# The expert down projection of two steps ends in one group of matmuls, in other row quarters

## The chip, the cores and the metric

The kernel runs on one core of a Trainium2 chip, as one launch. The metric is the device time of a run in microseconds (us); the time of before is the median of three runs.

## The reference

What is computed is a stack of six stages on 1024 tokens of width 512: a feed-forward block with retrieval, an attention, the same feed-forward block, a mixture of experts, a second attention, the mixture of experts again. The change touches the mixture of experts, which occurs twice:

```python
H, F, E, K = (512, 800, 8, 2)
...
top_vals, top_idx = jax.lax.top_k(probs, K)
...
h1 = jnp.einsum('th,efh->tef', xt, w1)
h3 = jnp.einsum('th,efh->tef', xt, w3)
act = jax.nn.silu(h1) * h3
expert_out = jnp.einsum('tef,ehf->teh', act, w2)
y = jnp.einsum('te,teh->th', w_full, expert_out)
```

Each token goes to 2 of 8 experts. An expert has 800 middle columns. All is float32.

## The kernel before

**Streams and steps.** The 2048 pairs of token and expert are sorted by expert and cut into blocks of 32 rows (`SR`), each of one expert. The blocks are dealt to four streams (`NSTR`), so that a stream has 18 steps (`NSTEP`), and one step handles four blocks, one of each stream. Stream j owns the column quarter j of TensorE's array (32 of its 128 columns) and the 32 PSUM partitions from 32j on. Both occurrences (f = 0 and f = 1) together have 36 steps.

**One step p**, over the engines:

- POOL: `gather(p)` (L880) is an indirect DMA that fetches 128 token rows from `h_scratch` into one of two slots of `XB`. Its wait is for the slot to be free. The scatter (L892) writes the step's 128 result rows from `YB` to `y_scratch`; it waits for `m_yc`, which the copy of the step raises. POOL's program is: gather(0), gather(1), then for each p: gather(p+2), wait for `m_yc` of step p, scatter of step p.
- DVE: `turn_rows(p)` (L1119) turns the gathered rows with 16 transposes. For step p its program is: `turn_rows(p+1)`, the two products of step p (L1125), the transposes of the activation of step p (L1138, L1141), which raise `m_at`.
- PE: `up(p)` (L954) multiplies by w1 and w3: 64 matmuls of 400 columns. It waits for `turn_rows(p)` (`m_xt`) and for both products of step p-1 (`m_act`), whose PSUM banks it writes. `down(p)` (L972, L975) multiplies by w2. The 800 middle columns are six chunks of 128 (`FC`), 24 matmuls of 512 columns at L972, and 32 left over (`FR`), 4 matmuls at L975 that use only 32 rows of the array, here called the tail. A step writes PSUM bank 4 or 5 (`4 + u`, u = p mod 2). PE's program is: up(0), up(1), down(0), up(2), down(1), up(3), down(2), and so on.
- ACT: silu of step p (L1001, two halves), then the copy of step p-1 from PSUM to `YB` (L1007), which waits for `m_y`, raised by the tail of that step, and raises `m_yc`.
- SP: issues the weight loads. A stream keeps its weights while its expert stays the same; the load is then skipped by a condition, but the instruction is still executed. `up_in` (L794) loads w1 and w3, `down_in` (L803) the chunks of w2, `tail_in` (L810) the 32 left-over rows of w2 (64 KB) into `W2B`. `down_in` and `tail_in` of a step raise one semaphore, `w2_in`, and wait for `m_y` of the step before.

Of the kernel before, what the change touches and what calls it, by code (L numbers as in the profile page):

```python
# [14 lines left out]
P = 128  # L15
T, D = 1024, 512
# [17 lines left out]
NE, FF, TOPK = 8, 800, 2  # L34
# [14 lines left out]
def macaron_program(nc, A, out, stages=6):  # L49

    ctx = ExitStack()
    with ctx:
# [159 lines left out]
        XBT = take([2, C, P])  # L212
        AC = take([FF])
        ACT_T = take([2, FC, P])
        ACT_R = take([2, SR])
        YB = take([2, D])
        W2B = take([D])
        W2_LAST = take([FC // 2, D])
        W13, W2A = [None] * NSTR, [None] * NSTR
        for j in (2, 0, 1):  # L220
# [565 lines left out]
        yl_in = [sem(f"yl_in{i}") for i in range(NT)]  # L786
        LOADS = NSTEP + 1
        N13 = 16 * NSTR
        N2 = 16 * (2 * NSTR + 1)
        assert NSTEP % 2 == 0  # L790

        def up_in(eng, j, a, e, cond=None):

# [11 lines left out]
                              cond=cond).then_inc(w2_in, 16)  # L805
                at += n

        def tail_in(eng, j, e, cond=None):

            eng.dma_start(W2B[SR * j:SR * j + SR], A["w2b"][e].rearrange("e p d -> p (e d)"),  # L810
                          cond=cond).then_inc(w2_in, 16)

        def guess(j):

# [8 lines left out]
        def sp_moe(eng, k, f):  # L823
            h, last = HS[k][0], 2 if f == 0 else 3
            for i in range(NT):
                eng.wait_ge(s_h, NT * k + i + 1)
                eng.dma_start(HD[i * P:(i + 1) * P, :], h[:, i, :]).then_inc(S("s_hd"), 16)
            eng.wait_ge(stage_end, 4 * k)
            for j in range(NSTR):
                tail_in(eng, j, guess(j))  # L830
            eng.wait_ge(S("s_hd"), 16 * NT * (f + 1))
            eng.wait_ge(S("s_lgt"), 4 * f + 4)
            guess_in(eng, f, last)

            eng.wait_ge(S("s_eb"), f + 1)
            late = None
            for p in range(NSTEP + 1):
                if p < NSTEP:
                    now = []
                    for j in range(NSTR):  # L840
                        q = j * NSTEP + p
                        x = eng.value_load(EBX[q:q + 1, 0:1], min_val=0, max_val=2 * NE - 1)
                        now.append((bass.ds(x % NE, 1), x >= NE))
                    for a in range(2):
                        if p == 0:
                            eng.wait_ge(w13_in[a], N13 * (LOADS * f + 1))
                        elif a == 0:
                            eng.wait_ge(S("m_wf"), NSTEP * f + p)
                        else:
                            eng.wait_ge(S("m_h"), 2 * (NSTEP * f + p))  # L850
                        for j in range(NSTR):
                            up_in(eng, j, a, *now[j])
                if p >= 1:
                    if p == 1:
                        eng.wait_ge(w2_in, N2 * (LOADS * f + 1))
                    else:
                        eng.wait_ge(S("m_y"), NSTEP * f + p - 1)
                    for j in range(NSTR):
                        down_in(eng, j, *late[j])
                        tail_in(eng, j, *late[j])  # L860
                late = now
            if f == 0:
                sp_attn1_weights(eng)
            for u in range(2):
                eng.wait_ge(y_out[u], 8 * NSTEP * (f + 1))
            for i in range(NT):
                rows_back(eng, i, 0)
# [29 lines left out]
        def pe_moe(eng, k, f):  # L897
# [65 lines left out]
            def down(p):  # L963
                G, u = NSTEP * f + p, p % 2
                eng.wait_ge(w2_in, N2 * (LOADS * f + p + 2))
                eng.wait_ge(S("m_at"), G + 1)
                if G >= 2:
                    eng.wait_ge(S("m_yc"), G - 1)
                for c in range(FC):
                    for j in range(NSTR):  # L970
                        part = W2A[j][c // W2A[j][0].shape[1]]
                        eng.matmul(PS[SR * j:SR * j + SR, 4 + u, :], ACT_T[:, u, c, SR * j:SR * j + SR],  # L972
                                   part[:, c % part.shape[1], :], start=(c == 0), stop=False, skip_group_check=True)
                for j in range(NSTR):
                    mm = eng.matmul(PS[SR * j:SR * j + SR, 4 + u, :], ACT_R[SR * j:SR * j + SR, u, :],  # L975
                                    W2B[SR * j:SR * j + SR, :], start=False, stop=True, skip_group_check=True)
                mm.then_inc(S("m_y"), 1)

            for p in range(NSTEP):
                up(p)  # L980
# [7 lines left out]
        def act_moe(eng, link, k, f):  # L988
            eng.wait_ge(S("s_fall"), f + 1)
            eng.activation(LESS, FALL, ACT.Exp).then_inc(S("s_less"), 1)  # L990
            eng.wait_ge(S("s_xturn"), f + 1)
            eng.copy(XBT[:, 0], PS[:, 6, :].rearrange("p (c t) -> p c t", c=C)).then_inc(S("m_xfirst"), 1)

            for p in range(NSTEP + 1):
                G = NSTEP * f + p
                if p < NSTEP:
                    for hf in range(2):
                        eng.wait_ge(S("m_h"), 2 * G + hf + 1)
                        if G > 0:
                            eng.wait_ge(S("m_at"), G)  # L1000
                        eng.activation(AC[:, hf * FH:(hf + 1) * FH], PS[:, 2 * hf, 0:FH], ACT.Silu).then_inc(S("m_sg"), 1)  # L1001
                if p >= 1:
                    u = (p - 1) % 2
                    eng.wait_ge(S("m_y"), G)
                    if p >= 3 or f == 1:
                        eng.wait_ge(y_out[u], 16 * (NSTEP // 2 * f + (p - 1) // 2))
                    eng.copy(YB[:, u, :], PS[:, 4 + u, :]).then_inc(S("m_yc"), 1)  # L1007
            for u in range(2):
                eng.wait_ge(y_out[u], 8 * NSTEP * (f + 1))
            for i in range(NT):  # L1010
                rows_back(eng, i, 1)
            if f == 0:
                for i in range(NT):
                    act_front(eng, k + 1, i)

        def dve_moe(eng, link, k, f):
# [110 lines left out]
            for p in range(NSTEP):  # L1127
                G, u = NSTEP * f + p, p % 2
                if p + 1 < NSTEP:
                    turn_rows(p + 1)  # L1130
                product(G, 0)
                product(G, 1)
                eng.wait_ge(S("m_act"), 2 * G + 2)
                if G >= 2:
                    eng.wait_ge(S("m_y"), G - 1)
                for a in range(NSTR):
                    rows = slice(SR * a, SR * a + SR)
                    eng.transpose(ACT_R[rows, u, :], AC[rows, FC * P:FF])  # L1138
                    for b in range(NSTR):
                        src = AC[rows, 0:FC * P].rearrange("p (c f) -> p c f", c=FC)  # L1140
                        tr = eng.transpose(ACT_T[SR * b:SR * b + SR, u, :, rows], src[:, :, SR * b:SR * b + SR])  # L1141
                tr.then_inc(S("m_at"), 1)
# [548 lines left out]
```

## Time and profile before

| | |
|---|---|
| median of 3 runs | 1366.42 us (1364.42 to 1369.72) |
| profiled execution: its time, its span | 1372.15 us, 1370.4 us |
| mean granted TensorE clock | 0.937 |
| PE busy | 1185.6 us, 87% of the span |
| DVE, ACT, POOL busy | 866.3, 350.0, 123.5 us |
| PE at L954 / L972 / L975 on the chain that ended last | 28% / 13% / 2% |

The span runs from the first to the last instruction of the profiled execution, and 1.75 us lie around it. The chain that ended last is followed back from the last instruction, at each step to what released it. A float32 matmul shows as two records, so a tail of four matmuls has 8. Line numbers are those of the kernel before; the first occurrence of the experts lies at about 195 to 545 us, the second at about 990 to 1368 us.

### The profile page before, as it was taken

The page shows a single profiled execution, that of the slowest core. Times are in us where ns is not written, and L with a number is a line of the kernel's source. Part 1 is how long each engine was busy: PE and PEld are TensorE (multiplying, and loading weights), DVE is VectorE, ACT ScalarE, POOL GpSimd, SP SyncE. Part 2 cuts the span into 40 slices and gives each one's busy share as a digit, 9 for nine tenths or more (in the row PEclk, how much of TensorE's full clock was granted, in tenths as well). Part 3 has the DMA queues.
Part 4 walks back from the last instruction along what each step waited for, and adds up shares of the span by engine and source line. Part 5 has one row for each costly group of instructions (what it writes and reads, how often), then busy time and mean ns, then how long its engine had stood idle before and what let it go on. Part 6 is the DMA issues. An engine that isn't in the chain of part 4 may idle for free.

```text
span 1370.4 us, 26531 instructions
## 1 busy us (share of the span) xinstructions
PE 1185.6 (87%) x9782; PEld 486.0 (35%) x9782; DVE 866.3 (63%) x2491; ACT 350.0 (26%) x723; POOL 123.5 (9%) x151
## 2 busy tenths in 40 slices
PE   6799756999999994688789999999759889999982
PEld 3477422333333331333334444433323323333320
DVE  4731476767787763654888888841358657777753
ACT  4434420000000000121166666674100000000000
POOL 1100010111111100220100000000100111111100
PEclk9899887999999997799999999999869999999995
DMA  9000332047503244239514331005640533514545
GB/s 368 11 1 1 142 137 99 32 175 280 216 33 128 94 155 170 94 101 128 101 42 78 58 56 29 2 2 215 279 167 17 224 123 138 185 65 140 179 179 206
DMA packets 44521, 166.15 MB, mean 121 GB/s; under 512 B 7613, under 2 KB 14355, under 8 KB 40039
## 3 DMA queue, kind: packets, MB, share of 16 engines
q1 hardware_dynamic: 34415, 137.28, 30.3%
q0 software_dynamic: 5760, 18.88, 4.0%
q10 hardware_dynamic: 4216, 8.29, 2.7%
q8 instruction: 77, 1.26, 0.4%
q14 instruction: 53, 0.43, 0.1%
HBM read 786.00 MB, written 22.03 MB: 590 GB/s over the span
## 4 chain that ended last, share of the span: by engine, by line
PE 75%; DVE 12%; DMA 5%; issue 3%; ACT 3%; SPq 1%; POOL 1%; ACTq 0%; POOLq 0%; DVEq 0%
PE PS L954 28%; PE PS L972 13%; PE PS L1397 5%; PE PS L1360 4%; PE PS L1384 4%; DVE PS L1519 3%; PE PS L975 2%; PE PS L706 2%; PE PS L689 2%; PE PS L1424 2%; PE PS L1343 2%; PE PS L479 2%; PE PS L493 1%; DMA HH<-in_w 1%; PE PS L1348 1%
## 5 line engine op out<-in xcount | busy, mean ns | idle before, releaser
L954 PE MATMUL PS<-arena 128*32 128x400 f32 x3456 | 399.0, 504 | 8.0 <-DMA HH<-in_w 4.0
L954 PE MATMUL PS<-HH,arena 128*32 128x400 f32 x1152 | 398.5, 504 | 0.0
L1119 DVE STREAM_TRANSPOSE arena<-arena 32x128 f32<-32x128 f32 x544 | 164.7, 303 | 144.8 <-DMA arena<-h_scratch,RT 137.6
L954 PEld LDWEIGHTS PS<-arena 128*32 128x32 f32 x3456 | 141.4, 111 | 261.7 <-issue 257.2
L1519 DVE CUSTOM_DVE_ANT_0 PS<-PS,U 128x128 f32<-128x128 f32 (+7 forms) x256 | 188.0, 783 | 59.3 <-PE PS L1360 58.5
L1141 DVE STREAM_TRANSPOSE arena<-arena 32x192 f32<-32x192 f32 x576 | 211.4, 367 | 7.2
L972 PE MATMUL PS<-arena 128*32 128x512 f32 x1512 | 197.7, 604 | 15.0 <-DMA arena<-in_w2b 15.0
L1465 ACT ACTIVATE arena<-PS 128x512 f32<-128x512 f32 (+3 forms) x384 | 165.2, 496 | 74.0 <-PE PS L1387 48.4
L1001 ACT ACTIVATE arena<-PS 128x400 f32<-128x400 f32 x72 | 36.3, 504 | 363.4 <-PE PS L954 363.4
L954 PEld LDWEIGHTS PS<-HH,arena 128*32 128x32 f32 x1152 | 124.6, 111 | 0.0
L1360 PE MATMUL PS<-arena 96*128 96x512 bf16 (+3 forms) x384 | 104.0, 332 | 17.6 <-DVE arena L1519 13.7
L1384 PE MATMUL PS<-arena 99*128 99x512 bf16 (+3 forms) x384 | 111.9, 330 | 5.1 <-DVE arena L1503 2.2
L972 PEld LDWEIGHTS PS<-arena 128*32 128x32 f32 x1512 | 55.9, 112 | 142.9 <-issue 125.2
L972 PE MATMUL PS<-HH,arena 128*32 128x512 f32 x216 | 104.2, 621 | 0.0
L892 POOL DMA_INDIRECT y_scratch<-arena,RT x36 | 35.7, 991 | 573.7 <-ACT arena L1007 573.7
L1397 PE MATMUL PS<-arena 128*32 128x512 f32 (+3 forms) x768 | 80.2, 497 | 0.0
L1007 ACT COPY arena<-PS 128x512 f32<-128x512 f32 x36 | 21.1, 586 | 223.9 <-PE PS L975 223.9
L479 PE MATMUL PS<-ident,HH 128*128 128x128 f32 x128 | 29.0, 382 | 53.7 <-DVE HH L454 52.7
L1343 PE MATMUL PS<-HH,arena 128*128 128x512 f32 x128 | 63.6, 622 | 0.8 <-ACTq L158 0.8
L1360 PEld LDWEIGHTS PS<-arena 96*128 96x128 bf16 x384 | 31.3, 99 | 92.1 <-DVE arena L1519 62.8
L1125 DVE TENSOR_TENSOR arena<-arena,PS 128x400 f32<-128x400 f32 x72 | 39.3, 569 | 34.4 <-ACT arena L1001 33.1
L1384 PEld LDWEIGHTS PS<-arena 99*128 99x128 bf16 x384 | 37.1, 98 | 55.5 <-ACT arena L1465 34.1
(246 smaller groups left out, 1156.3 us busy)
## 6 DMA issues: line engine op xcount, KB each, us to landing
arena<-in_w SPq DMA_DIRECT2D x228, 1600.0 KB
arena<-in_w2a SPq DMA_DIRECT2D x114, 1536.0 KB
HH<-in_w SPq DMA_DIRECT2D x76, 1600.0 KB
HH<-in_w2a SPq DMA_DIRECT2D x38, 768.0 KB
arena<-in_w2a SPq DMA_DIRECT2D x38, 768.0 KB
arena<-in_w2b SPq DMA_DIRECT2D x152, 64.0 KB
arena<-split_scratch SPq DMA_DIRECT2D x72, 128.0 KB, 6.5
split_scratch<-arena SPq DMA_DIRECT2D x48, 128.0 KB, 2.3
```

The source lines that it names most:

```text
L479: tr = eng.transpose(PS[:, FB[k][i % 2], c * P:(c + 1) * P], HS[k][0][:, i, c * P:(c + 1) * P], ident[:])
L954: mm = eng.matmul(PS[SR * j:SR * j + SR, 2 * hf + m, 0:FH], XBT[:, u, c, SR * j:SR * j + SR], W13[j][:, c // 2, m, c % 2, hf * FH:(hf + 1) ...
L972: eng.matmul(PS[SR * j:SR * j + SR, 4 + u, :], ACT_T[:, u, c, SR * j:SR * j + SR], part[:, c % part.shape[1], :], start=(c == 0), stop=Fal ...
L1119: tr = eng.transpose(XBT[SR * b:SR * b + SR, u, :, SR * a:SR * a + SR], src[:, :, SR * b:SR * b + SR])
L1125: eng.tensor_tensor(half, half, PS[:, 2 * hf + 1, 0:FH], ALU.mult).then_inc(S("m_act"), 1)
L1141: tr = eng.transpose(ACT_T[SR * b:SR * b + SR, u, :, rows], src[:, :, SR * b:SR * b + SR])
L1343: mm = eng.matmul(PS[:, at + par, :], wcols[:, par], HS[k][1][:, c, J * HT_:(J + 1) * HT_], start=(c == 0), stop=(c == C - 1))
L1360: mm = eng.matmul(PS[:, b + lo // HT_, 0:hi - lo], QT[0:KS, slot, h, i * P:(i + 1) * P], KT[0:KS, slot, h, lo:hi], start=True, stop=True)
L1384: mm = eng.matmul(bank[:, 0:hi - lo], KT[0:KS + 3, slot, h, i * P:(i + 1) * P], QT[0:KS + 3, slot, h, lo:hi], start=True, stop=not diag, s ...
L1397: mm = eng.matmul(PS[32 * h:32 * h + 32, 7, lo - J * HT_:HT_], VA[:, i, (GH * g + h) * VC:(GH * g + h) * VC + 32], PB[:, n % 3, h, 0:hi - lo],
L1465: eng.activation(PB[:, (n // GH) % 3, h, 0:hi - lo], PS[:, 4 + n % 3, 0:hi - lo], ACT.Exp, scale=SCALE1).then_inc(S("s_p"), 1)
L1519: eng.tensor_tensor_reduce(scores, scores, MASKW[:, T - wide:T], 1.0, HOLE, ALU.add, ALU.max, MP[:, g % 2, h, i:i + 1]).then_inc(S("s_md"), 1)
```

## The change

The tail of an even step is not multiplied in its own `down`. It waits for the tail of the odd step after it, and both are multiplied together, 8 matmuls in turn: those of the even step in row quarter j and column quarter j, those of the odd step in row quarter j+1 (mod 4) and column quarter j, with results in banks 4 and 5. So it is for steps 0 to 15; steps 16 and 17 (`not paired`) each end with a tail of their own. What follows from it in the code:

- `ACT_R` (the left-over columns of the activation) has 4 slots instead of 2, `W2B` two buffers, one of them in `U`, which is free in this stage.
- The last L972 matmul of each step raises a new semaphore `m_w2`; `down_in` and the DVE transposes wait for that instead of `m_y`. `m_y` rises by two at the tail of a pair.
- `tail_in` comes behind all `down_in` of a step, has semaphores of its own (`w2b_in`) and no condition: 4 x 64 KB at each step.
- ACT copies both steps of a pair one after the other, behind the silu of the step after the pair.
- POOL's program, with its waits, is not edited.

```diff
-        ACT_R = take([2, SR])
+        ACT_R = take([4, SR])
         YB = take([2, D])
-        W2B = take([D])
+        W2B = [take([D]), U]
...
+        def paired(p):
+
+            return p < NSTEP - 2
+
+        def y_done(p):
+
+            return p + 2 if paired(p) and p % 2 == 0 else p + 1
+
+        def last_rows(p, j):
+
+            r = (j + p % 2) % NSTR
+            return slice(SR * r, SR * r + SR)
...
-        def tail_in(eng, j, e, cond=None):
-
-            eng.dma_start(W2B[SR * j:SR * j + SR], A["w2b"][e].rearrange("e p d -> p (e d)"),
-                          cond=cond).then_inc(w2_in, 16)
+        def tail_in(eng, p, j, e):
+
+            eng.dma_start(W2B[p % 2][last_rows(p, j)], A["w2b"][e].rearrange("e p d -> p (e d)")).then_inc(w2b_in[p % 2], 16)
...
                 if p >= 1:
-                    if p == 1:
+                    q = p - 1
+                    if q == 0:
                         eng.wait_ge(w2_in, N2 * (LOADS * f + 1))
                     else:
-                        eng.wait_ge(S("m_y"), NSTEP * f + p - 1)
+                        eng.wait_ge(S("m_w2"), NSTEP * f + q)
                     for j in range(NSTR):
                         down_in(eng, j, *late[j])
-                        tail_in(eng, j, *late[j])
+                    if q >= 2:
+                        eng.wait_ge(S("m_y"), NSTEP * f + y_done(q - 2))
+                    for j in range(NSTR):
+                        tail_in(eng, q, j, late[j][0])
...
+                mm.then_inc(S("m_w2"), 1)
+                if paired(p) and p % 2 == 0:
+                    return
+                ends = (p - 1, p) if paired(p) else (p,)
+                for q in ends:
+                    eng.wait_ge(w2b_in[q % 2], N2B * (NSTEP // 2 * f + q // 2 + 1))
                 for j in range(NSTR):
-                    mm = eng.matmul(PS[SR * j:SR * j + SR, 4 + u, :], ACT_R[SR * j:SR * j + SR, u, :],
-                                    W2B[SR * j:SR * j + SR, :], start=False, stop=True, skip_group_check=True)
-                mm.then_inc(S("m_y"), 1)
+                    for q in ends:
+                        rows = last_rows(q, j)
+                        mm = eng.matmul(PS[SR * j:SR * j + SR, 4 + q % 2, :], ACT_R[rows, (NSTEP * f + q) % 4, :],
+                                        W2B[q % 2][rows, :], start=False, stop=True, skip_group_check=True)
+                mm.then_inc(S("m_y"), len(ends))
...
-                if p >= 1:
-                    u = (p - 1) % 2
-                    eng.wait_ge(S("m_y"), G)
-                    if p >= 3 or f == 1:
-                        eng.wait_ge(y_out[u], 16 * (NSTEP // 2 * f + (p - 1) // 2))
+                if p >= 1 and not paired(p - 1):
+                    ready = (p - 1,)
+                elif p >= 2 and p % 2 == 0:
+                    ready = (p - 2, p - 1)
+                else:
+                    ready = ()
+                for q in ready:
+                    u = q % 2
+                    eng.wait_ge(S("m_y"), NSTEP * f + y_done(q))
+                    if q >= 2 or f == 1:
+                        eng.wait_ge(y_out[u], 16 * (NSTEP // 2 * f + q // 2))
                     eng.copy(YB[:, u, :], PS[:, 4 + u, :]).then_inc(S("m_yc"), 1)
```

On PE, before, at the end of down(0) of the first occurrence (the last chunks, the tail, the first matmuls of up(2)); down(1) ends in the same way:

```order
L972 MATMUL PS<-arena 32x512 x3
L972 MATMUL PS<-HH,arena 32x512
L972 MATMUL PS<-arena 32x512 x12
L975 MATMUL PS<-arena 32x512 x4
L954 MATMUL PS<-arena 32x400 x3
```

and of the change, first at the end of down(0) (L989 and L971 are the lines of before's L972 and L954):

```order
L989 MATMUL PS<-arena 32x512 x3
L989 MATMUL PS<-HH,arena 32x512
L989 MATMUL PS<-arena 32x512 x12
L971 MATMUL PS<-arena 32x400 x3
L971 MATMUL PS<-HH,arena 32x400
```

then at the end of down(1) (L1000 is the line of before's L975, `U` the second buffer of left-over rows):

```order
L989 MATMUL PS<-arena 32x512 x12
L1000 MATMUL PS<-arena 32x512
L1000 MATMUL PS<-U,arena 32x512
L1000 MATMUL PS<-arena 32x512
L1000 MATMUL PS<-U,arena 32x512
L1000 MATMUL PS<-arena 32x512
L1000 MATMUL PS<-U,arena 32x512
L1000 MATMUL PS<-arena 32x512
L1000 MATMUL PS<-U,arena 32x512
L971 MATMUL PS<-arena 32x400 x3
```

The four tail matmuls of down(0) have moved behind down(1), in turn with its own.

On ACT, from the first silu of the experts on, before (two silu halves a step, then a copy):

```order
L1001 ACTIVATE arena<-PS 128x400 x4
L1007 COPY arena<-PS 128x512
L1001 ACTIVATE arena<-PS 128x400 x2
L1007 COPY arena<-PS 128x512
L1001 ACTIVATE arena<-PS 128x400 x2
L1007 COPY arena<-PS 128x512
```

and of the change (L1026 is the silu, L1038 the copy):

```order
L1026 ACTIVATE arena<-PS 128x400 x6
L1038 COPY arena<-PS 128x512 x2
L1026 ACTIVATE arena<-PS 128x400 x4
L1038 COPY arena<-PS 128x512 x2
```

The copy of step 0 has moved from behind the silu of step 1 to behind that of step 2, next to the copy of step 1.

On POOL the order is the same before and after; here it is from the first gathers on (L880 is a gather, the first three are those of steps 0, 1 and 2; L892 is a scatter, of steps 0, 1 and 2):

```order
L880 DMA arena<-h_scratch,RT 128x512 x3
L892 DMA y_scratch<-arena,RT 4353x512
L880 DMA arena<-h_scratch,RT 128x512
L892 DMA y_scratch<-arena,RT 4353x512
L880 DMA arena<-h_scratch,RT 128x512
L892 DMA y_scratch<-arena,RT 4353x512
```

Nothing moved here: the gather of step 3 stands behind the scatter of step 0.

## Rows read from the trace of the kernel before

**Rows 1.** The page: span, busy time of the engines.

```profile
span 1370.4 us, 26531 instructions
PE 1185.6 (87%) x9782; PEld 486.0 (35%) x9782; DVE 866.3 (63%) x2491; ACT 350.0 (26%) x723; POOL 123.5 (9%) x151
```

**Rows 2.** Chain that ended last, steps of the first occurrence: start us, us, what.

```profile
299.46 10.88 PE PS L954 x128
310.34 5.15 PE PS L972 x48
315.49 0.99 PE PS L975 x8
316.48 10.88 PE PS L954 x128
```

**Rows 3.** Timeline of PE, down(4) and the start of up(6): start us, us, what.

```profile
310.16 0.61 PE L972 MATMUL PS<-arena 128*32 128x512 f32 x3
...
310.59 0.60 PE L972 MATMUL PS<-arena 128*32 128x512 f32 x3
...
314.88 0.61 PE L972 MATMUL PS<-arena 128*32 128x512 f32 x4
315.42 1.06 PE L975 MATMUL PS<-arena 32*32 32x512 f32 x8
316.41 0.54 PE L954 MATMUL PS<-arena 128*32 128x400 f32 x3
```

**Rows 4.** Timeline of ACT, the copy of step 4: idle time before in brackets.

```profile
316.55 0.59 ACT L1007 COPY arena<-PS 128x512 f32<-128x512 f32 x1 [5.64 <-PE PS L975]
```

**Rows 5.** Timeline of POOL, same place: scatter of step 4, gather of step 7.

```profile
317.41 0.99 POOL L892 DMA_INDIRECT y_scratch<-arena,RT  x1 [14.76 <-ACT arena L1007]
318.71 0.97 POOL L880 DMA_INDIRECT arena<-h_scratch,RT  x1 [0.30 <-issue]
```

**Rows 6.** Timeline of DVE, turn_rows(7) and, a step on, turn_rows(8) and both products.

```profile
322.08 5.05 DVE L1119 STREAM_TRANSPOSE arena<-arena 32x128 f32<-32x128 f32 x16 [1.86 <-DMA arena<-h_scratch,RT]
...
328.57 0.20 DVE L1138 STREAM_TRANSPOSE arena<-arena 32x32 f32<-32x32 f32 x1
...
333.91 1.53 DVE L1141 STREAM_TRANSPOSE arena<-arena 32x192 f32<-32x192 f32 x4
342.91 5.05 DVE L1119 STREAM_TRANSPOSE arena<-arena 32x128 f32<-32x128 f32 x16 [7.48 <-DMA arena<-h_scratch,RT]
348.00 1.05 DVE L1125 TENSOR_TENSOR arena<-arena,PS 128x400 f32<-128x400 f32 x2
```

**Rows 7.** Waits, longest first: who waited for whom, us in total, times, longest.

```profile
POOL y_scratch L892 <- ACT arena L1007: 573.7, 36, 30.9
...
DVE arena L1119 <- DMA arena<-h_scratch,RT: 137.6, 28, 8.6
```

**Rows 8.** The gathers at L880 between 383 and 440 us, few weight loads.

```profile
DMA to landing us min/median/max: 3.2/3.3/4.0
```

**Rows 9.** The same between 330 and 372 us, amid weight loads.

```profile
DMA to landing us min/median/max: 7.0/7.2/7.6
```

**Rows 10.** Chain that ended last: pieces of PE that follow an idle time of PE.

```profile
217.71 12.29 PE PS L954 x128
...
523.99 7.05 PE PS L972 x48
...
1015.69 12.65 PE PS L954 x128
...
1118.42 6.90 PE PS L972 x48
```

**Rows 11.** Windows around PE's wait at down(17) of the second occurrence.

```profile
core 0: us, PE busy (x) PEld busy (x) DVE busy (x) ACT busy (x) POOL busy (x), PEclk, DMA share, GB/s
...
1330.67:1338.62 7.95, 0.00 (x0) 0.00 (x1) 1.79 (x6) 0.59 (x1) 0.99 (x1) 0.66 0.69 240
1338.62:1343.40 4.78, 4.78 (x24) 1.17 (x28) 0.00 (x0) 0.00 (x0) 0.00 (x0) 0.50 0.00 0
```

**Rows 12.** Chain that ended last: weight transfers that PE waited for, second occurrence.

```profile
1076.61 15.43 DMA HH<-in_w
...
1108.20 10.17 DMA arena<-in_w2b
```

**Rows 13.** Timeline of SP after down(16) of the first occurrence: first, second and last issue.

```profile
521.08 0.07 SPq L803 DMA_DIRECT2D arena<-in_w2a  x1
521.43 0.07 SPq L810 DMA_DIRECT2D arena<-in_w2b  x1
...
523.89 0.07 SPq L810 DMA_DIRECT2D arena<-in_w2b  x1
```

**Rows 14.** Timeline of PE: the first records of down(17), first and second occurrence, and of down(4), second.

```profile
523.99 0.88 PE L972 MATMUL PS<-arena 128*32 128x512 f32 x3 [3.21 <-DMA arena<-in_w2b]
...
1118.42 1.07 PE L972 MATMUL PS<-arena 128*32 128x512 f32 x3 [3.73 <-DMA arena<-in_w2b]
...
1338.62 1.07 PE L972 MATMUL PS<-arena 128*32 128x512 f32 x3 [8.02 <-DMA arena<-in_w2b]
```

More of the change, by code:

```diff
@@ L788, in macaron_program @@
         N13 = 16 * NSTR
-        N2 = 16 * (2 * NSTR + 1)
+        N2 = 16 * (NSTR + 1)
+        N2B = 16 * NSTR
+        w2b_in = [sem("w2b_in0"), sem("w2b_in1")]
         assert NSTEP % 2 == 0
+        def paired(p):
[5 more added lines that the diff above has]
+            return slice(SR * r, SR * r + SR)
         def up_in(eng, j, a, e, cond=None):
@@ L828, in sp_moe @@
             eng.wait_ge(stage_end, 4 * k)
-            for j in range(NSTR):
-                tail_in(eng, j, guess(j))
             eng.wait_ge(S("s_hd"), 16 * NT * (f + 1))
@@ L971, in down @@
                         part = W2A[j][c // W2A[j][0].shape[1]]
-                        eng.matmul(PS[SR * j:SR * j + SR, 4 + u, :], ACT_T[:, u, c, SR * j:SR * j + SR],
-                                   part[:, c % part.shape[1], :], start=(c == 0), stop=False, skip_group_check=True)
-                for j in range(NSTR):
-                    mm = eng.matmul(PS[SR * j:SR * j + SR, 4 + u, :], ACT_R[SR * j:SR * j + SR, u, :],
-                                    W2B[SR * j:SR * j + SR, :], start=False, stop=True, skip_group_check=True)
-                mm.then_inc(S("m_y"), 1)
+                        mm = eng.matmul(PS[SR * j:SR * j + SR, 4 + u, :], ACT_T[:, u, c, SR * j:SR * j + SR],
+                                        part[:, c % part.shape[1], :], start=(c == 0), stop=False, skip_group_check=True)
+                mm.then_inc(S("m_w2"), 1)
[4 more added lines that the diff above has]
+                    eng.wait_ge(w2b_in[q % 2], N2B * (NSTEP // 2 * f + q // 2 + 1))
+                for j in range(NSTR):
+                    for q in ends:
[3 more added lines that the diff above has]
+                mm.then_inc(S("m_y"), len(ends))
             for p in range(NSTEP):
@@ L1134, in dve_moe @@
                 if G >= 2:
-                    eng.wait_ge(S("m_y"), G - 1)
+                    eng.wait_ge(S("m_w2"), G - 1)
                 for a in range(NSTR):
                     rows = slice(SR * a, SR * a + SR)
-                    eng.transpose(ACT_R[rows, u, :], AC[rows, FC * P:FF])
+                    eng.transpose(ACT_R[last_rows(p, a), G % 4, :], AC[rows, FC * P:FF])
                     for b in range(NSTR):
```

## The prediction

> **What bounds the kernel now.** I read the page first: PE is busy for 1185.6 of 1370.4 us [rows 1]. A busy share alone does not say that PE sets the pace, so I read the chain of work that ended last. In a steady step of the experts it is PE from end to end: 10.88 us of up, 5.15 us of chunks, 0.99 us of tail, and the next up at once [rows 2]. A step is 17.02 us and no other engine is on the chain. So what PE no longer does in a steady step is won, as long as everything PE waits for still comes in time. That makes two questions: what does the tail cost PE, and who is fed by the tail's end?
>
> **What the tail costs PE.** The chunks of down(4) start at 310.16, the second pass at 310.59: a pass of four concurrent matmuls takes 0.43 us. The last chunk pass starts at 314.88, the tail at 315.42, up(6) at 316.41 [rows 3]. Without the tail, up(6) would start one pass after 314.88, at 315.30 (up follows chunks, and chunks follow up, without a loss). The tail therefore costs 316.41 - 315.30 = 1.1 us, of which two passes are 0.85 and 0.26 is lost at the two changes between 128-row and 32-row matmuls.
>
> **What the change removes.** 16 even steps (8 pairs in each occurrence) lose their tail: 16 x 1.1 = 18 us, if the pair's tail takes no longer than a single one. That is not in the trace: in the tail of before the four matmuls differ in row quarter and column quarter [rows 3], in the pair's two share each column quarter. Bounds: at best the eight overlap as the four do, 0 more; at worst the pair runs as two groups of four, 0.85 us more, 14 us in all. I take 0, because the nearest row is the diagonal tail, which overlaps fully, and the two of a column quarter write different banks. The 14 stay for the range.
>
> **What it moves, and who waits for it.** The end of the tail releases ACT's copy, and the copy releases POOL. In before's trace, take T = 316.41, where down(4) has ended and up(6) begins. The copy of step 4 starts at 316.55 [rows 4], POOL's scatter at 317.41, and behind it in POOL's program the gather, at 318.71 [rows 5]. By the order of POOL this gather is that of step 7, not of step 5 or 6: gather(p+2) stands behind the scatter of step p-1. POOL spends its time in just this wait, 573.7 us in 36 waits [rows 7]. Now it costs nothing: gather(7) lands as turn_rows(7) starts, at 322.08 [rows 6], and up(7) begins one step of 17.02 us after up(6), at 333.4.
>
> After the change the copy of an even step comes only after the tail of the pair, one step later. POOL isn't edited, so the gather of step p+3 (p even, so an odd step) moves with the copy by a step. The pair (4, 5) ends with down(5), and what stands next on PE is up(7), which needs gather(7). The gather is issued when PE already wants its product. All pairs do this: gather(3) behind the copy of step 0, which now follows down(1), directly ahead of up(3), up to gather(17) ahead of up(17); 8 stalls in each occurrence, 16 in all.
>
> **Length of one stall**, from the moment T when the pair's down has ended:
>
> - copy, scatter and issue of the gather: 318.71 - 316.41 = 2.30 us [rows 3 to 5].
> - gather to landing, L: 3.3 us in a quiet stretch [rows 8], 7.2 amid weight loads [rows 9].
> - turn_rows: 5.05 us, 16 transposes [rows 6].
> - DVE has turn_rows(7) ahead of the products of step 6 in its program, so these, which before ran while PE was in down, now come after it. up(7) waits for both, since they free its PSUM banks: 1.05 us [rows 6], and about 0.1 for handing over.
>
> Together 8.5 + L. For L both ends are in the trace. Between them: the quiet gather (3.35 us, 318.71 to 322.06) makes DVE wait 1.86 us [rows 6]; the mean wait over the run is 137.6 / 28 = 4.9 us [rows 7], which would make L at most 3.35 + 3.05 = 6.4 in the mean. The 28 leave out the gathers for which DVE did not wait at all, and part of the extra is DVE being early. I take 4.7, a third of the gathers amid loads: a stall of 13.2 us, between 11.8 and 14.9.
>
> Nothing covers it. PE has neither down(6) (it needs the transposes of step 6, which need the products) nor up(7). The other gather (step 8) is issued right behind the second scatter, and is turned during up(7), so even steps don't stall. After the stall, transposes(6) (6.9 us, from 328.57 to 333.91 + 1.53 in a steady step [rows 6]) end well inside up(7).
>
> **The clock after a stall.** [...] Four other pieces that follow a wait show the price against their steady 10.88 or 5.15 us: +1.4, +1.9, +1.8, +1.75 [rows 10]; their idle times reach down to 3.2 us [rows 14]. A stall of 13 us is longer than all of these, so I take 1.8 for each, bounds 1.4 and 2.4 (half of 4.78).
>
> **Smaller edits.** (a) In the second occurrence down(4) waited 3.73 us for its w2 transfer [rows 12, 14], and ran 1.75 us slow. Its load starts with the end of down(3); now up(5) stalls 13 us in between, and covers it: -5.4 us. The other wait there, for the w1 and w3 transfer of 15.43 us [rows 12], starts in up(3), behind that stall, and stays; there the 1.1 of one even tail is lost, and about as much gained, since a scatter and a gather no longer share the transfer's time. (b) down(17) waits for SP's nine issues at 0.35 us each, 521.08 to 523.89, in the first occurrence [rows 13], for the transfer in the second [rows 14]. `down_in` now starts at the end of the chunks, and the tails' issues come later: about 1.2 us won at each, -2.4. (c) Unconditional `tail_in`: 256 KB a step, where a skipped one took 0.35 us of SP's time [rows 13] and a real one takes some tenths more. SP reaches its next wait about 1 us later, at worst beside the middle of an up; the step that this feeds is an odd one, and lies behind a stall. Without that cover it could cost up to 1 us in the steps with loads. The pair waits for `w2b_in` some 16 us after the issue of the earlier one and 10 after the later: hidden. (d) The second copy, 0.59 us, lies in ACT's idle time (5.64 us ahead of a copy [rows 4]); DVE's transposes are as many as before.
>
> **Sum.** Per pair: 13.2 + 1.8 - 1.1 = +13.9 us; 16 pairs: +222. Less 5.4 and 2.4: +214 us. The profiled execution would go from 1370.4 to 1584 us of span, with the 1.75 around it 1586 against 1372.15. The median shown is 5.7 us under the profiled execution; on it the same difference gives 1366.4 + 214 = **1581 us**.
>
> **Rivals.**
>
> - *The gather is in time, only PE's saving counts.* This ends on the other side: 1366.4 - 18 - 2.4 = 1346 us. It decides where gather(p+3) is issued at least 6.2 + L, so 9.5 us ahead of the end of the pair's down. For it: before, the same gather is issued 14.7 us ahead of its up (17.02 - 2.30), 5 more than it needs. Against: POOL's wait is a count of copies in step order, and the first copy of a pair lies behind the tail at the pair's very end. 3 in 100.
> - *The rule on banks.* If matmuls in different row quarters could not write one bank together, the pair's 16 records, four row quarters to a bank, would run one by one: 16 x 0.43 = 6.9 us instead of 0.85, +97 us over 16 pairs, 1678 in all. The trace speaks against it: before's tail has four row quarters in one bank, 8 records in 1.06 us [rows 3]. [...] 2 in 100.
> - *The paired tail doesn't overlap in a column quarter*, so the change doesn't do on PE what it says: two groups of four, +14, 1595 us. 12 in 100.
> - *Every gather lands late.* With all L at 7.2, the stall is 15.7 us and the sum 16 x (15.7 + 1.8 - 1.1) - 8 = +254, 1620 us. The even gathers of before that fall at an odd down's end are partly in quiet stretches [rows 8], so not all. 7 in 100.
> - *No change within 0.5%*: needs a stall of about 1 us instead of 13. 1 in 100.
>
> My forecast has the remaining 75.
>
> **How the numbers follow.** Low end of the forecast: 16 x (11.8 + 1.4 - 1.1) - 8 = +186, 1552. High end: 16 x (14.9 + 2.4 - 1.1) - 8 = +251, 1618. The 1595 lies inside; 1346, 1678 and 1620 with what is above it are left out. Range 1550 to 1618. 0.5% is about what a measurement of this kernel can tell from no change (1359.6 to 1373.3 us). Faster 0.03, within 0.5% 0.01, slower 0.96.
>
> **What would show it.** Right, if in the profile of the changed kernel (1) PE waits for DVE's products or the gather's turn 16 times, each ahead of an odd up from 3 to 17, some 12 to 15 us long; (2) the gather of an odd step is issued some 2.3 us after the end of an odd down; (3) a pair of steps takes 46 to 48 us instead of 34; (4) the clock is 0.5 for some 3 to 5 us behind each stall; (5) L989 chunks of an even step are followed by up without a gap, and the pair's tail takes 1.1 us. A stall some us longer or shorter than 13.2 would be L. If the odd gathers are found issued early, or a stall covered by other work of PE, the prediction is wrong as a whole.

## Result: 16.7% slower

The changed kernel takes 1595.74 us (median of 4 runs, 1594.07 to 1600.89) against 1366.3 us (now the median of 4 runs of before): ratio 1.1671, 95% interval 1.1642 to 1.1700. The prediction was 1581 us, range 1550 to 1618. The profiled execution took 1594.4 us with a span of 1592.6 us, 222 us more than before's span.

Two measures are used below. Ratios compare a kernel with runs of before made beside it. The median of before was 1366.3 to 1372.2 us in these sets of runs, so a difference in us between two medians of different sets is good to some 6 us. The second measure, "the two stages", leaves the rest of the program out: in the profiled execution, the time from PE's first record of up(0) to its last of down(17), both occurrences added. It is 646.0 us before and 870.2 us in the changed kernel, 224 us more.

The head of the page of the changed kernel:

```profile
span 1592.6 us, 26539 instructions
PE 1201.6 (75%) x9782; PEld 503.6 (32%) x9782; DVE 866.6 (54%) x2491; ACT 348.3 (22%) x723; POOL 123.3 (8%) x151
...
PE PS L971 27%; PE PS L989 11%; DMA arena<-h_scratch,RT 5%; DVE arena L1150 5%; PE PS L1428 4%; PE PS L1391 4%; PE PS L1415 3%; DVE PS L1550 2%; PE PS L706 2%; PE PS L689 2%; PE PS L1455 2%; PE PS L1374 2%; PE PS L479 1%; PE PS L1000 1%; POOL y_scratch L909 1%
```

PE is as busy as before but for 16 us [rows 1], and its share fell from 87% to 75%. The gathers (`h_scratch`) and the turn of their rows (L1150) are on the chain now with 5% each; before, neither was among its lines of 1% and more. The chain at the first two pairs of the first occurrence, the longer pieces (L971 is up, L989 the chunks, L1000 the tails, L1038 the copy, L909 the scatter, L1150 turn_rows):

```profile
237.75 5.15 PE PS L989 x48
242.90 10.75 PE PS L971 x128
253.64 5.15 PE PS L989 x48
258.79 1.10 PE PS L1000 x16
259.92 0.59 ACT arena L1038
260.78 1.01 POOL y_scratch L909
...
262.09 3.38 DMA arena<-h_scratch,RT
...
270.56 1.17 issue
271.73 12.33 PE PS L971 x128
...
305.11 1.10 PE PS L1000 x16
306.24 0.59 ACT arena L1038
307.10 0.99 POOL y_scratch L909
...
308.39 7.33 DMA arena<-h_scratch,RT
...
321.98 12.81 PE PS L971 x128
```

This answers to [rows 2]. The first two rows show PE's saving: up follows the chunks of the even step at once. Behind the pair's tail PE hands over to ACT, POOL, a transfer and DVE, and up(3) starts at 271.73, 12 us later; the second pair, whose gather took 7.3 us, waits for 16. The up behind each stall takes 12.3 and 12.8 us instead of 10.88. The "issue" of 1.17 us ahead of up is not a free stretch: DVE's row at that place shows the two products that up waits for. Here are DVE's, POOL's and PE's rows of the first stall, from their timelines:

```profile
265.50 5.05 DVE L1150 STREAM_TRANSPOSE arena<-arena 32x128 f32<-32x128 f32 x16 [18.86 <-DMA arena<-h_scratch,RT]
270.58 1.05 DVE L1156 TENSOR_TENSOR arena<-arena,PS 128x400 f32<-128x400 f32 x2
```

```profile
260.78 1.01 POOL L909 DMA_INDIRECT y_scratch<-arena,RT  x1 [47.10 <-ACT arena L1038]
262.09 0.97 POOL L897 DMA_INDIRECT arena<-h_scratch,RT  x1 [0.30 <-issue]
```

```profile
271.73 0.89 PE L971 MATMUL PS<-arena 128*32 128x400 f32 x3 [11.92 <-issue]
```

The clock behind the stall of up(15), second occurrence, by windows (columns as in [rows 11]):

```profile
1488.00:1493.10 5.10, 5.09 (x32) 1.77 (x36) 4.91 (x16) 0.00 (x0) 0.00 (x0) 0.50 0.02 3
1493.10:1501.20 8.10, 8.10 (x100) 3.20 (x96) 6.96 (x22) 0.50 (x1) 0.00 (x0) 1.00 0.01 3
```

The eight records of the paired tail's first pass, here the first and the last, start within 0.05 us:

```profile
258.72 0.61 PE L1000 MATMUL PS<-arena 32*32 32x512 f32 x1
...
258.77 0.61 PE L1000 MATMUL PS<-U,arena 32*32 32x512 f32 x1
```

And the waits of the whole run:

```profile
POOL y_scratch L909 <- ACT arena L1038: 793.3, 20, 47.8
...
DVE arena L1150 <- DMA arena<-h_scratch,RT: 351.5, 18, 30.7
PE PS L971 <- issue: 216.4, 18, 17.3
```

DVE waited 137.6 us for gathers before [rows 7], now 351.5. The difference, 214 us, is as large as PE's wait ahead of the 16 odd ups: 216.4 us in 18 times, of which two are 1.28 us at up(1).

### The profile page after: what moved, and what is told of

Read it like the earlier page. It is cut to its first block, busy times and chain, and to the rows that moved or that the text cites. A ratio compares the mean times of both kernels' runs of the same rounds, so it can differ in the third digit from the quotient of the medians.

```text
span 1592.6 us, 26539 instructions
## 1 busy us (share of the span) xinstructions
PE 1201.6 (75%) x9782; PEld 503.6 (32%) x9782; DVE 866.6 (54%) x2491; ACT 348.3 (22%) x723; POOL 123.3 (8%) x151
## 4 chain that ended last, share of the span: by engine, by line
PE 66%; DVE 15%; DMA 8%; issue 5%; ACT 3%; POOL 2%; SPq 1%; ACTq 0%; POOLq 0%; DVEq 0%
PE PS L971 27%; PE PS L989 11%; DMA arena<-h_scratch,RT 5%; DVE arena L1150 5%; PE PS L1428 4%; PE PS L1391 4%; PE PS L1415 3%; DVE PS L1550 2%; PE PS L706 2%; PE PS L689 2%; PE PS L1455 2%; PE PS L1374 2%; PE PS L479 1%; PE PS L1000 1%; POOL y_scratch L909 1%
## 5 line engine op out<-in xcount | busy, mean ns | idle before, releaser
L971 PE MATMUL PS<-arena 128*32 128x400 f32 x3456 | 433.1, 538 | 223.4 <-issue 216.4
L971 PE MATMUL PS<-HH,arena 128*32 128x400 f32 x1152 | 432.4, 538 | 0.0
L1150 DVE STREAM_TRANSPOSE arena<-arena 32x128 f32<-32x128 f32 x544 | 164.7, 303 | 358.9 <-DMA arena<-h_scratch,RT 351.5
L971 PEld LDWEIGHTS PS<-arena 128*32 128x32 f32 x3456 | 161.3, 117 | 493.2 <-issue 486.3
L989 PE MATMUL PS<-arena 128*32 128x512 f32 x1512 | 195.4, 599 | 8.6 <-DMA arena<-in_w2a 6.6
L1026 ACT ACTIVATE arena<-PS 128x400 f32<-128x400 f32 x72 | 36.2, 503 | 687.4 <-PE PS L971 687.4
L971 PEld LDWEIGHTS PS<-HH,arena 128*32 128x32 f32 x1152 | 133.1, 117 | 0.0
L1391 PE MATMUL PS<-arena 96*128 96x512 bf16 (+3 forms) x384 | 104.7, 334 | 17.6 <-DVE arena L1550 13.8
L989 PE MATMUL PS<-HH,arena 128*32 128x512 f32 x216 | 101.7, 608 | 0.0
L989 PEld LDWEIGHTS PS<-arena 128*32 128x32 f32 x1512 | 59.0, 111 | 131.4 <-issue 123.9
L909 POOL DMA_INDIRECT y_scratch<-arena,RT x36 | 35.6, 988 | 798.1 <-ACT arena L1038 793.3
L1418 PE MATMUL PS<-mask_st,identb 128*128 128x128 bf16 x256 | 53.3, 223 | 0.0
```

Source lines behind the costliest of these rows:

```text
L909: eng.indirect_dma_start(YS[:, :], bass.IndirectOffsetOnAxis(ap=SIDX[:, p:p + 1], axis=0), YB[:, p % 2, :], None).then_inc(y_out[p % 2], 16)
L971: mm = eng.matmul(PS[SR * j:SR * j + SR, 2 * hf + m, 0:FH], XBT[:, u, c, SR * j:SR * j + SR], W13[j][:, c // 2, m, c % 2, hf * FH:(hf + 1) ...
L989: mm = eng.matmul(PS[SR * j:SR * j + SR, 4 + u, :], ACT_T[:, u, c, SR * j:SR * j + SR], part[:, c % part.shape[1], :], start=(c == 0), sto ...
L1150: tr = eng.transpose(XBT[SR * b:SR * b + SR, u, :, SR * a:SR * a + SR], src[:, :, SR * b:SR * b + SR])
L1391: mm = eng.matmul(PS[:, b + lo // HT_, 0:hi - lo], QT[0:KS, slot, h, i * P:(i + 1) * P], KT[0:KS, slot, h, lo:hi], start=True, stop=True)
L1418: mm = eng.matmul(bank[:, 0:P], identb[:], mask_st[:], start=False, stop=True, skip_group_check=True)
```

## Experiments

**Only the copies delayed.** The kernel before, with ACT's copies in pairs and nothing else:

```diff
-                if p >= 1:
-                    u = (p - 1) % 2
-                    eng.wait_ge(S("m_y"), G)
+                if p >= 1 and p - 1 >= NSTEP - 2:
+                    ready = (p - 1,)
+                elif p >= 2 and p % 2 == 0:
+                    ready = (p - 2, p - 1)
+                else:
+                    ready = ()
+                for q in ready:
...
```

> The kernel before, with one edit on ACT: the copies of steps 2n and 2n+1 (up to step 15) are both made behind the silu of step 2n+2, so the copy of an even step comes one step later. PE, SP and DVE are those of before, with a tail at each step. My theory (the delay of the even step's copy is the whole cause): the same 16 stalls of about 13.5 us and 1.8 us of slow clock behind each, no saving on PE: 1366 + 16 x 15.3 - 5 = about 1606 us, some 10 to 18 us above the changed kernel's 1596. Rival (the delay of the copy alone is harmless, the pair's tail or its loads are needed for the stall): 1366 us.

Measured: 1594.11 us, ratio 1.1624 (1.1573 to 1.1676). The waits (here L1125 is `turn_rows`, before's L1119; L954 is up as before):

```profile
DVE arena L1125 <- DMA arena<-h_scratch,RT: 360.4, 18, 28.9
PE PS L954 <- issue: 209.6, 18, 15.9
```

The delayed copy alone brings the whole slowdown; neither the paired tail nor its loads are needed for it. It came 12 us below the expected 1606. In this run the slow up behind a stall was cheaper: L954 was busy for 428.3 us, 29 more than before, where in the changed kernel L971 was busy for 34 more; and PE waited 7 us less ahead of its ups (209.6 against 216.4). So the intervals of the two ratios overlap, though one kernel has PE's saving and the other not; in the two stages this one takes 874.2 us, 4 more than the changed kernel. Why its slow ups and its waits were a little shorter is left open.

**Only the gathers freed.** The changed kernel with POOL's program in another order, and the kernel before with the same edit as its base line:

```diff
-            gather(0)
-            gather(1)
+            for p in range(4):
+                gather(p)
             eng.wait_ge(S("s_sidx"), f + 1)
             for p in range(NSTEP):
-                if p + 2 < NSTEP:
-                    gather(p + 2)
+                if p % 2 == 0:
+                    for g in (p + 4, p + 5):
+                        if g < NSTEP:
+                            gather(g)
```

> The changed kernel, with POOL's program alone rewritten: the gathers of steps 0 to 3 come first, then before the scatters of each pair (p, p+1) the gathers of steps p+4 and p+5, which wait only for their slot. My theory (the added time is the odd step's gather behind the pair's first scatter): the 16 stalls and the slow clock behind them go, PE's saving stays, 16 x 1.1 us and some 2.4 at the two ends: 1346 us, ratio to before 0.985. Rival 1 (the paired tail or the loads of the left-over rows themselves cost the time): it stays near 1590. Rival 2 (only part of it is the gather, the pair also brings other waits): between 1366 and 1400.

> The kernel before, with the same rewritten order of gathers on POOL as in the first experiment and nothing else. It is the base line for it. My theory: before the change the gather's landing was hidden behind the up of a step, so nothing is won, 1366 us, within 0.3% of before. Rival (the gathers amid weight loads already cost PE something): up to some 5 us faster.

Measured: with pairs 1352.58 us, ratio 0.9895 (0.9869 to 0.9921); the base line 1370.43 us, ratio 1.0008 (0.9993 to 1.0023). The slowdown is gone, so it was the gather's place in POOL's program. The base line shows that early gathers win nothing by themselves; the 1% belongs to the pairs and the smaller edits that come with them (the run without pairs, below, tells these apart). The chain of the version with pairs in its undisturbed stretch (L973 is up, L991 the chunks, L1002 the tails):

```profile
455.55 5.15 PE PS L991 x48
460.70 1.02 PE PS L1002 x16
461.72 10.88 PE PS L973 x128
472.60 5.15 PE PS L991 x48
477.75 10.75 PE PS L973 x128
488.50 5.15 PE PS L991 x48
493.65 1.02 PE PS L1002 x16
```

A pair of steps takes 32.95 us from tail to tail instead of 2 x 17.02, 1.09 less. But I had expected 0.985, 6 us more than was measured. In the two stages 16.0 us are won (646.0 to 630.0) where about 20 were expected. PE's waits for weights in this kernel, beside which stand 15.0 and 4.0 us for the two in the kernel before:

```profile
PE PS L991 <- DMA arena<-in_w2a: 9.7, 2, 6.4
PE PS L973 <- DMA HH<-in_w: 7.8, 5, 5.0
```

The first fell, by the earlier start of `down_in`. The second grew from 2 waits to 5. Of the growth of 3.8 us, 1.8 are there without pairs too: the two waits of up(4), second occurrence, take 5.8 us in the run without pairs. The other 2.0 are three new waits of 0.35, 0.53 and 1.10 us in the first occurrence: with the tail gone from an even step, its next up comes 1.1 us earlier and meets weights that are not there yet. The two groups together still fell, from 19.0 to 17.5 us, so the waits account for 1 us of what is missing against the expected 2.4 us won; the rest is not traced to a place. The chain ahead of one of the three (L819 is down_in, L855 the register loads that tell the step's experts; tail_in lies between them, up_in behind):

```profile
260.25 0.13 SPq L819
...
264.24 0.35 SPq L855
...
268.83 8.65 DMA HH<-in_w
277.48 0.14 issue
277.61 10.95 PE PS L973 x128
```

SP begins its work at the end of the chunks, and needs 8.6 us until the last `up_in` is issued.

**SP's register loads earlier.** They were moved right behind `up_in` of the step before, on top of the freed gathers, with pairs and without:

```diff
...
                         for j in range(NSTR):
                             up_in(eng, j, a, *now[j])
+                    ahead = experts(p + 1) if p + 1 < NSTEP else None
                 if p >= 1:
...
```

> The first experiment (pairs, early gathers) and one more edit on SP: the four register loads that tell a step's experts are made right behind the up_in of the step before, ahead of the waits of down_in and tail_in, instead of behind them. In the first experiment an even step's shorter time laid SP's program open: up of an even step waited for its weights 0.4 to 1.1 us in three steps of the first occurrence and 5 us in step 4 of the second, and the chain led back over tail_in and these register loads (2.6 us) to the chunks' end. My theory: the weight loads start up to 1 us earlier, the three short waits go and the long one shrinks by some 1 us: 3 us less than the first experiment's ratio of 0.9895, so about 0.987 of before. Rival (the transfers' own rate sets these waits): no change, 0.9895.

> The kernel before with both edits of the run beside it, early gathers on POOL and early register loads on SP, and no pairs: the base line for it. My theory: SP was nearly in time before, so at most some 1 us is won at step 4 of the second occurrence: ratio 0.998 to 1.000. Rival: it wins as much as the version with pairs, and the pairs are worth nothing: 0.987.

Measured: with pairs 1350.96 us, ratio 0.9858 (0.9827 to 0.989); without 1367.93 us, ratio 0.9984 (0.9964 to 1.0004). PE's waits for w1 and w3 went from 7.8 us in 5 times to 5.2 in 4 (L979 is up, L997 the chunks):

```profile
PE PS L997 <- DMA arena<-in_w2a: 9.8, 2, 6.5
PE PS L979 <- DMA HH<-in_w: 5.2, 4, 2.3
```

The step from 0.9895 to 0.9858 is some 5 us where 3 were expected, but the intervals overlap, and in the two stages of the profiled execution it is 0.7 us (630.0 to 629.3). That the waits became shorter is shown; that the kernel became faster is not. Against its base line, the pairs with their smaller edits are worth about 1.3%, in the two stages 16.2 us (645.5 to 629.3). This version has the lowest ratio of all, below both kernels; from the version with freed gathers alone it can't be told.

**The same row quarter.** As the version with freed gathers, but with both tails of a pair in row quarter j:

```diff
-            r = (j + p % 2) % NSTR
+            r = j
```

> As the first experiment (pairs, early gathers), but both tails of a pair use row quarter j and column quarter j, so that two matmuls of a pair need the same 32 x 32 part of the array. My theory (the pair overlaps because its row quarters differ): two more passes of 0.43 us in each of 16 pairs, 0.85 x 16 = 14 us over the first experiment, 1360 us. Rival (the order of issue alone lets them overlap, or what is saved is mainly the change between 128 and 32 rows): the same time as the first experiment, 1346.

Measured: 1363.03 us, ratio 0.9959 (0.9944 to 0.9975). The tails in this kernel's chain:

```profile
257.81 1.87 PE PS L1002 x16
```

1.87 us instead of 1.02: the two passes more that were expected, 13.6 us over 16 pairs. About 9 us of it arrive, in the ratio and in the two stages (630.0 to 639.0): 6.5 of 6.8 in the first occurrence, 2.6 of 6.8 in the second, where this execution lost less around step 4: down(4) took 5.36 us for its chunks instead of 7.05. The different row quarters are what lets the pair overlap.

**No pairs, all other edits kept.**

```diff
-            return p < NSTEP - 2
+            return False
```

> The changed kernel with paired(p) false for every step: each step has its own tail again and its copy at once, but the other edits stay (m_w2, the tails' loads unconditional, behind down_in and with semaphores of their own, two buffers, four slots, the odd step's tail in row quarter j+1). POOL as before. My theory (these edits cost nothing where PE is the bound, and save about 1.2 us at each of the two last steps, up to 2 more where down(4) waits for its transfer): 1363 us, ratio 0.997. Rival (the 256 KB at each step or SP's longer program delay weight loads): 1370 to 1380 us.

Measured: 1365.16 us, ratio 0.9975 (0.9954 to 0.9996), as expected. The unconditional loads of 256 KB a step, the two buffers and `m_w2` together cost nothing; they win 0.25%, 1.9 us in the two stages (644.1). The pairs alone are then worth 644.1 - 630.0 = 14.1 us there, 12.6 between the two medians, which were taken beside each other. This run has POOL's old order of gathers, which the base line above showed to make no difference.

**The stall filled with 36, then with 50 matmuls.** Behind the tail of each pair of the changed kernel:

```diff
                 mm.then_inc(S("m_y"), len(ends))
+                if paired(p):
+                    for n in range(36):
+                        eng.matmul(PS[:, 6, 0:P], ident[:], ones[:], start=True, stop=True, skip_group_check=True)
```

Measured with 36: 1591.5 us, ratio 1.1602 (1.155 to 1.1655), a miss by 25 us; in the two stages it is 871.1 us, as much as in the changed kernel. PE's rows at the first stall (L1005 is the filler):

```profile
260.58 8.30 PE L1005 MATMUL PS<-ones,ident 128*128 128x128 f32 x72
273.01 0.89 PE L971 MATMUL PS<-arena 128*32 128x400 f32 x3 [4.12 <-issue]
```

They took 0.23 us each, not 0.29, and 4.1 us of idle time stayed ahead of up, whose first record still has the slow duration (0.89 us; 0.54 where the granted clock is 1.00); over its first 3 us the granted clock was 0.50. So I filled the rest:

> As the experiment that filled the stalls with 36 matmuls of 128 x 128, now with 50. The 36 took 8.3 us and left PE idle for about 4 us at each stall, and the clock still fell in 15 of 16. 50 take 11.5 us and leave under 1 us in the eleven stalls of about 12 us, 3 to 6 in the five longer ones. My theory (what counts is the idle stretch ahead of up): in the eleven the clock stays at its full level and each saves the 2.2 us that the slow up cost in the changed kernel, 24 us in all: about 1571 us. Rival (these matmuls do not hold the clock at all): about 1592, as with 36.

Measured with 50: 1569.16 us, ratio 1.1466 (1.142 to 1.1513).

```profile
260.34 11.43 PE L1005 MATMUL PS<-ones,ident 128*128 128x128 f32 x100
272.40 0.54 PE L971 MATMUL PS<-arena 128*32 128x400 f32 x3 [0.64 <-issue]
```

The first record of up is back at 0.54 us, and the granted clock was 1.00 over its first 6 us. And the chain of this kernel at the first four stalls, x128 rows being up(3), up(5), up(7), up(9):

```profile
272.40 10.95 PE PS L971 x128
...
321.93 13.22 PE PS L971 x128
...
372.64 13.46 PE PS L971 x128
...
422.79 12.29 PE PS L971 x128
```

The first stall is filled, the next three are longer than the filler by 3 to 5 us, and there the slow up stayed (granted clock 0.50, 0.50 and 0.54 over the first 3 us). Over the whole run the up takes 10.95 us behind ten stalls (eleven were expected), and 12.3 to 13.5 behind the other six. The slow clock is thus a price of its own: L971 is busy for 410.8 us instead of 433.1, 22 less, and the two stages take 848.7 us, also 22 less, though six stalls still pay it. (The medians differ by 27 us, but they come from different sets of runs.)

**Products ahead of the turn.** The changed kernel; on DVE, in the even steps from 2 on, the two products come before `turn_rows` of the next step:

```diff
-                if p + 1 < NSTEP:
+                late_turn = p >= 2 and p % 2 == 0
+                if p + 1 < NSTEP and not late_turn:
                     turn_rows(p + 1)
                 product(G, 0)
                 product(G, 1)
+                if p + 1 < NSTEP and late_turn:
+                    turn_rows(p + 1)
```

> The changed kernel with DVE's program of the even steps from 2 on in another order: the two products of the step come before turn_rows of the next step instead of behind it. My theory (in a stall PE waits for gather, turn_rows and then the products, one after the other): each stall is shorter by the products' 1.1 us, 16 x 1.1 = 18 us less, 1578 us. Rival (the products were not on the way, since up's wait for them is met earlier): 1596 us.

Measured: 1574.41 us, ratio 1.1474 (1.1424 to 1.1525), 21 us less than the changed kernel by the medians of two sets, 14.5 in the two stages (855.8). PE's wait ahead of up is now put down to the turn of the rows:

```profile
PE PS L971 <- DVE arena L1150: 196.2, 16, 16.0
```

196.2 / 16 = 12.3 us, 1.1 less than in the changed kernel, 17.6 in all; the ups took 2.9 us more (L971 busy for 436.0 us). The products were the last link of the chain, hidden in its profile under "issue".

## Why the prediction was right, and where it was off

- **The mechanism** holds as forecast: gather(p+3) stands behind the scatter of step p, whose copy now comes a step later. The delayed copies alone make the slowdown, and the freed gathers alone remove it.
- **Length of a stall**: 13.2 us predicted. Measured (216.4 - 2.6) / 16 = 13.4. Its links are as read: copy to gather's issue 262.09 - 259.89 = 2.2, gather 3.4 to 8.8 (on average 13.4 - 8.5 = 4.9 for the assumed 4.7), turn 5.05, products 1.05 and the handing over. It is 12.3 where the products go first.
- **The clock** was sized too low: 1.8 us a stall predicted. L971 was busy for 433.1 us, L954 for 399.0 before, 34 us or 2.1 a stall; the single ups behind a stall took 12.3 to 13.8 us on the chain. The prediction averaged four rows [rows 10]. The piece behind the longest wait, 8.02 us [rows 14], went only into the upper bound of 2.4 (half of the 4.78 us at a granted clock of 0.50 [rows 11]), though it is the nearest to a stall: there the chunks of down(17) ran from 1338.62 to the tail's first record at 1346.27, 7.65 us for 5.15, 2.5 more.

```profile
1346.27 1.06 PE L975 MATMUL PS<-arena 32*32 32x512 f32 x8
```

  A longer wait does not make the price higher in the changed kernel: behind its longest stall, 17.3 us, the up took 12.33 us, and behind those of 11.9 to 12.4 us it took 12.3 to 13.6. What sets it between these ends is open.
- **PE's saving**: 1.1 us a pair predicted. An even step is 5.15 + 10.75 us where it was 5.15 + 0.99 + 10.88, so 1.12 are saved; the pair's tail takes 1.10 or 1.02 us instead of 0.99. About 1.0 is left. (The 1.10 runs to the end of the last record, which counts where PE stands idle behind it; with freed gathers up follows after 1.02, and 1.09 are left.) The doubt about overlap in a column quarter is settled: it overlaps (1.02 us on the chain with freed gathers), and with the same row quarter it does not (1.87).
- **The rival on banks** did not come true: in different column quarters, matmuls of different row quarters wrote one bank at the same time. Eight records of four row quarters, each 0.61 us long, start within 0.05 us of each other, four in each of two banks, and the 16 of a pair took 1.10 us, not 6.9. Whether two row quarters of one column quarter could share a bank was not tried.
- **Smaller edits**: down(4) of the second occurrence no longer waits for weights, as forecast. The wait of up(4) for w1 and w3, put at no change, grew from 4.0 to 5.6 us. The waits at the two down(17) fell from 3.2 to 2.0 and from 8.0 to 6.6 us, for 1.2 us each predicted. SP's later reach was put at up to 1 us a step with loads, if the cover of the stalls were gone. With freed gathers the waits for w1 and w3 grew by 3.8 us, of which the run without pairs has 1.8; the other 2.0 come with the shorter even step.
- **The sum**: 16 x (13.4 + 2.1 - 1.0) - 5.4 - 2.6 = +224 us, for 224 measured in the two stages, 222 between the two spans and 229 between the medians. I had +214. Of the 15 us missing at the median, 5 are the clock, 3 the stall, 2 the pair's tail; the rest is the difference between medians and profiled executions, which I took to be the same in both kernels: before, the profiled execution lay 5.9 us above the median, after, 1.3 below it.

## What to carry to other kernels

Before an engine's result is held back to be handled in pairs, follow the semaphore that it raises through every in-order program that waits for it: here a copy that PE itself waits for only at the chunks of two steps later, to have its bank free, stood ahead of the load of PE's next rows, in the program of an engine with a busy share of 9%. A load that needs only a free buffer should not stand behind a store that needs a result. With the loads moved ahead, the same pairing with its smaller edits wins 1.1 to 1.3% against the base lines; and once PE's step is shorter, the next thing to look at is the program of the engine that issues the weights.

## What the runs showed of the hardware

- The pair's tail is eight float32 matmuls of 32 rows, 32 columns and 512 moving columns, in eight different 32 x 32 parts of the array. It took 1.02 us on the chain of the version with freed gathers and 1.10 in the changed kernel; the four matmuls of a single tail took 0.99 [rows 2]. With both matmuls of a column quarter in one part (the run with the same row quarter) it took 1.87.
- With 36 filling matmuls, 8.3 us of them and then 3.8 to 9.6 us without any stood ahead of the 16 ups behind a stall. In 15 of them the mean granted clock was 0.50 to 0.61 over the first 3 us; in the 16th, behind 3.81 us without, it was 1.00 over the first 6 us. With 50 of them, which took 11.4 us, it was 1.00 over the first 6 us in the ten ups that had at most 2.1 us without any ahead of them, and 0.50 to 0.55 over the first 3 us in the six that had 3.3 to 6.2 us.
- In two of the 15 (474.04 and 1531.86 us) the second pass of up (a pass is four concurrent records) still started 0.34 and 0.33 us behind the first, and soon after passes came 0.65 to 0.67 us apart. The mean granted clock was 0.81 over the first 0.56 us of the one and 1.00 over the first 0.44 us of the other, and 0.72 over the first 6 us of both.
- In the changed kernel the granted clock was 0.50 to 0.53 over the first 3 us of the ups behind a stall, and they were 1.4 to 2.9 us longer than 10.88. In up(15) a pass followed the pass before by 0.67 us where it was 0.50 (1491.31 to 1491.98) and by 0.34 where it was 1.00 (1493.56 to 1493.90). By these two numbers the ups ran for 3 to 6 us at 0.50, an estimate; the window at up(15) shows it for 5.1 us.
